# The selective stage: normalisation on ScalarE, modulation on GpSimd, and the network's end in the next turn

## The reference, cut to what is computed here

```python
def _L3_xattn_ref(x_text, x_vision, ...):        # x_text = _layernorm(x)
    Q = (x_text @ Wq).reshape(Bb, Tt, H, DH)      # 4 heads of 32
    K = (x_vision @ Wk).reshape(Bb, Gg, H, DH)
    scores = jnp.einsum('bthd,bghd->bhtg', Q, K) / np.sqrt(DH).astype(np.float32)
    topv, topi = jax.lax.top_k(scores, K_TOP)     # 32 of 120
    probs = jax.nn.softmax(topv, axis=-1)
    attn = jnp.zeros_like(scores).at[bi, hi, ti, topi].set(probs)
    attn_mean = attn.mean(axis=1)
    V = x_vision @ Wv
    c_t = jnp.einsum('btg,bgd->btd', attn_mean, V)
    x = layernorm(x_text, g_norm_in, b_norm_in)
    scale_in, shift_in = jnp.split(c_t @ W_film_in + b_film_in, 2, axis=-1)
    x = x * (1.0 + mod_gate * scale_in) + mod_gate * shift_in
    y = s4d(x, log_dt, A_re, A_im, C_re, C_im, D_skip)
    scale_out, shift_out = jnp.split(c_t @ W_film_out + b_film_out, 2, axis=-1)
    y = y * (1.0 + mod_gate * scale_out) + mod_gate * shift_out
    xt = x_text + y
    h = layernorm(xt, g_ffn, b_ffn)
    h = jax.nn.gelu(h @ W1 + b1, approximate=False) @ W2 + b2
    xt = xt + h
    return layernorm(xt, g_norm_out, b_norm_out)
```

## Time and profile before

| | us |
|---|---|
| median of 3 runs (lowest, highest) | 4631.86 (4628.33, 4635.73) |
| the profiled execution | 4636.67 |
| its span | 4634.9 |
| TensorE busy in the span | 4151.4 (90%) |
| VectorE busy | 3322.0 (72%) |
| ScalarE busy | 2232.4 (48%) |
| GpSimd busy | 529.9 (11%) |

### The profile page before, as it was taken

How to read it: one execution, slowest core, us unless ns; L and a number is a source line. 1 busy time by engine, 2 the same in 40 slices (tenths; PEclk the granted TensorE clock), 3 DMA queues, 4 the chain that set the end, 5 groups by cost and what they waited for, 6 DMA issues and landing times. The chain is left out here.

```text
span 4634.9 us, 72082 instructions
## 1 busy us (share of the span) xinstructions
PE 4151.4 (90%) x23376; PEld 3267.9 (71%) x23376; DVE 3322.0 (72%) x7934; ACT 2232.4 (48%) x5314; POOL 529.9 (11%) x982
## 2 busy tenths in 40 slices
PE   7998988999699999999999999999985888888686
PEld 6876766777387877778777777777863665656555
DVE  6985667666677777777777677777767888876455
ACT  3545655555365565655555555565531232322332
POOL 1331010111500000000000000001142111111300
PEclk9998999999799999999999999999975999989699
DMA  3000000000000000000000000000020000000101
GB/s 93 0 0 37 0 1 0 0 0 0 18 3 2 4 2 4 1 2 4 2 4 2 4 1 2 4 2 2 1 72 1 1 1 0 0 1 0 40 0 36
DMA packets 33797, 40.58 MB, mean 9 GB/s; under 512 B 5550, under 2 KB 30006, under 8 KB 33466
## 3 DMA queue, kind: packets, MB, share of 16 engines
q1 hardware_dynamic: 32732, 37.03, 2.7%
q10 hardware_dynamic: 800, 0.33, 0.0%
HBM read 32.90 MB, written 4.19 MB: 8 GB/s over the span
## 5 line engine op out<-in xcount | busy, mean ns | idle before, releaser
L1739 ACT ACTIVATE global_prob_t_high<-psum 128x512 fp32r<-128x512 f32 x960 | 570.7, 601 | 588.9 <-PE psum L1853 588.9
L1647 DVE TENSOR_TENSOR global_prob_t_low<-psum,global_prob_t_high 128x512 fp32r<-128x512 f32 x960 | 657.2, 690 | 251.0 <-ACT global_prob_t_high L1739 237.0
L1653 DVE TENSOR_REDUCE global_top<-psum 128x1 f32<-128x480 f32 x1024 | 666.9, 658 | 110.8 <-PE psum L1813 106.3
L1811 PE MATMUL psum<-global_prob_t_high,global_v_low 128*128 128x512 f32 x960 | 455.6, 475 | 1.0
L1811 PE MATMUL psum<-global_k_high,global_q_low 128*128 128x480 f32 x1024 | 390.6, 381 | 17.4 <-ACT spare L1760 14.8
L1813 PE MATMUL psum<-global_k_high,global_q_high 128*128 128x480 f32 x1024 | 391.1, 382 | 0.0
L1812 PE MATMUL psum<-global_k_low,global_q_high 128*128 128x480 f32 x1024 | 388.9, 380 | 0.0
L1812 PE MATMUL psum<-global_prob_t_low,global_v_high 128*128 128x512 f32 x960 | 379.7, 396 | 0.0
L1813 PE MATMUL psum<-global_prob_t_high,global_v_high 128*128 128x512 f32 x960 | 379.6, 395 | 0.0
L1760 ACT ACTIVATE spare<-psum,global_bias 128x480 f32<-128x480 f32 x512 | 337.8, 664 | 16.5 <-DVE global_bias L1656 15.1
L1760 ACT ACTIVATE global_prob<-psum,global_bias 128x480 f32<-128x480 f32 x512 | 337.9, 663 | 1.2
(11 more groups left out here) (455 smaller groups left out, 8593.3 us busy)
## 6 DMA issues: line engine op xcount, KB each, us to landing
x_res<-in_x SPq DMA_DIRECT2D x8, 512.0 KB, 9.8
moe_we<-in_expert_t SPq DMA_DIRECT2D x8, 512.0 KB, 7.6
out<-x_res SPq DMA_DIRECT2D x4, 1024.0 KB, 8.5
cho_wqkv<-in_L_ffn_Wqkv SPq DMA_DIRECT2D x2, 1536.0 KB
self_ctx_t<-in_ctx_t SPq DMA_DIRECT2D x2, 1440.0 KB, 13.6
sel_w<-in_L_xattn_W SPq DMA_DIRECT2D x2, 1024.0 KB, 11.2
global_ctx_t<-in_ctx_t SPq DMA_DIRECT2D x1, 1440.0 KB
sel_ctx_t<-in_ctx_t SPq DMA_DIRECT2D x1, 1440.0 KB
```

The lines of the kernel that those rows point to most:

```text
L1647: dve.tensor_tensor(dst, psum, high.bitcast(F32), ALU.subtract).then_inc(ready.sem, 1)
L1653: ins = dve.tensor_reduce(top[:, c:c + 1], w.psum[:, c, 0:chunk], AX.X, ALU.max)
L1739: act.activation(dst, psum, ACT.Copy).then_inc(ready.sem, 1)
L1811: pe.matmul(to, lhs_low, rhs_high, start=start, stop=False)
```

## The change

In one turn there is now a fourth sequence, done (now - 1), and one more turn at the end.

- **Layernorm of x, h and the last one.** VectorE still makes the statistics. GpSimd makes the root and beside it `offset` = -mean * root. ScalarE then normalises with one activation a tile (`Identity`, scale = root, bias = offset). It was VectorE before.
- **Second layernorm (g_norm_in).** The statistics of the normalised rows are no longer taken: their mean is nought, and their variance is var * root^2, from which GpSimd takes the second root (`rstd_of_normed`). VectorE multiplies xl by it and by the gain, and adds the bias row.
- **Modulation of u** (two operations of 128x512): GpSimd in place of VectorE, ahead of the sum with shift_out in its order.
- **The network's end** (sum over W2's result, statistics, normalisation, gain, sum into x): at the start of the next turn on VectorE, in place of the end of this one.
- **TensorE's order**: k and v, transposes of the mean, forward, transposes of xl, c, q, backward, scores, film_in, transposes of h, W1, W2, film_out.
- **ScalarE's order**: the exponentials ahead of the gelus.

```diff
+            iteration((2 * t + 2, 0), (2 * t + 1, 1), (2 * t, 0), 2 * t - 1)
+            iteration((2 * t + 3, 1), (2 * t + 2, 0), (2 * t + 1, 1), 2 * t)
+        iteration(None, (B - 1, 1), (B - 2, 0), B - 3)
+        iteration(None, None, (B - 1, 1), B - 2)
+        iteration(None, None, None, B - 1)
...
     def scale_rows(pool, chain, half, n):
-        _, mean_var, r = norms[half]
+        _, mean_var, r, offset = norms[half]
         need(pool, f"stats_{half}", n)
+        pool.tensor_tensor(offset[:, :], mean_var[:, :, 0], minus_one[:, :], ALU.mult)
         chain.link(pool.tensor_tensor(r[:, :], mean_var[:, :, 1], w.eps[:, :], ALU.add))
-        pool.tensor_tensor(r[:, :], r[:, :], w.neg_half[:, :], ALU.pow).then_inc(sig(f"rstd_{half}").sem, 1)
+        chain.link(pool.tensor_tensor(r[:, :], r[:, :], w.neg_half[:, :], ALU.pow))
+        pool.tensor_tensor(offset[:, :], offset[:, :], r[:, :], ALU.mult).then_inc(sig(f"rstd_{half}").sem, 1)
+
+    def scale_normed_rows(pool, chain):
+        _, mean_var, r, _ = norms["a"]
+        r2 = rstd_of_normed[:, :]
+        chain.link(pool.tensor_tensor(r2, mean_var[:, :, 1], r[:, :], ALU.mult))
+        chain.link(pool.tensor_tensor(r2, r2, r[:, :], ALU.mult))
+        chain.link(pool.tensor_tensor(r2, r2, w.eps[:, :], ALU.add))
+        pool.tensor_tensor(r2, r2, w.neg_half[:, :], ALU.pow).then_inc(sig("rstd_normed").sem, 1)
...
                 if F:
                     i, p = F
+                    need(pool, "u_base", i)
+                    need(pool, "film_in_ready", i)
+                    chain.link(pool.tensor_tensor(u_in[p], u_in[p], mods_in[:, :, 0:D], ALU.mult))
+                    pool.tensor_tensor(u_in[p], u_in[p], mods_in[:, :, D:2 * D],
+                                       ALU.add).then_inc(sig("u_ready").sem, 1)
                     need(pool, "film_out_ready", i)
...
+                if done is not None:
+                    need(dve, "ffn_psum", done)
+                    link(dve.tensor_tensor(xt, w.psum[:, 4:6, 0:D], xt, ALU.add))
+                    dve.engine_nop().then_inc(sig("ffn_kept").sem, 1)
+                    stats("b", 2 * done + 1, lambda s: xt[:, s, :])
                 if T:
-                    stats("a", 2 * T[0], x_tile(T[0]))
+                    stats("a", T[0], x_tile(T[0]))
+                if done is not None:
+                    need(dve, "yn_ready", done)
+                    link(dve.tensor_tensor(y, y, rows["g_norm_out"][:, :].unsqueeze(1).to_broadcast([P, LANES, D]),
+                                           ALU.mult))
+                    need(dve, "x_biased", done)
+                    dve.tensor_tensor(both_tiles(done), both_tiles(done), y, ALU.add).then_inc(sig("x_updated").sem, 1)
...
+            def normalise(half, x, to):
+                _, _, r, offset = norms[half]
+                for s in range(LANES):
+                    ins = act.activation(to[:, s, :], x(s), ACT.Identity, scale=r[:, s:s + 1], bias=offset[:, s:s + 1])
+                return ins
```

200 lines of the change are left out of this document (94 added, 106 removed).

## The result

The changed kernel takes 4577.85 us (median of four runs, 4572.24 to 4580.45) against 4632.74 us (4628.33 to 4635.73) for the kernel before: a ratio of 0.9881, 95% interval 0.9864 to 0.9898. It is 54.9 us, or 1.2%, faster. The forecast was 4617 us with a range of 4597 to 4640, so the direction was right and the gain was 3.7 times the expected one (54.9 against 14.9).

A forecast was written before the change was run, and what follows sets the result against it. Bound: a chain back and forth between TensorE and VectorE. From 4636.67, -17 for 13 turns, -4 ahead and +6.5 at the end give 4622.2 us profiled, so a forecast of 4617 us, range 4597 to 4640.

The forecast's parts named there:

- The removed waits: TensorE's waits for ffn_kept, xl and ScalarE's copies go; its matmuls stay the same, 36.50 us a turn.
- The cover over h: Scores and film_in on TensorE stand over h's normalisation, some 5.3 us, with 0.1 to 0.3 us to spare.
- The wait at the head: TensorE stands 3.3 us before kv each turn, behind film_out's copies, base and the context's copy.
- W2: TensorE's W2 waits 1.15 us a turn because ScalarE's exponentials now stand ahead of the gelus.
- Backward's: A term of 0.15 us in the sum for TensorE's turn at full clock, 41.8 us.
- The clock: After the head's wait, kv, mean's transposes and forward run at 1.2 GHz: 3.4 us lost, turns of 45.2.
- First and last turns: Outside the 13 full turns: -4 us ahead of the first W1, +6.5 us at the end.
- (a): Rival: the head costs no more clock than now; turns of 43.9 us or less, median 4595 to 4607; chance 0.20.
- (b): Rival: ScalarE's table loads, exponentials and gelus become the bound; turns 45.8 to 46.5, median 4625 to 4635; chance 0.23.
- (c): Rival: 1.2 GHz lasts past forward over c, q and backward; 12 us of it make median 4651; chance 0.12.
- (d): Rival: VectorE still sets the head, yn or products late; 1 us late makes turns of 46.2; chance within (b)'s.
- room of 0.7 us at full clock: At the head, the products are through 11.1 us after film_out and TensorE wants the spectrum at 11.8.

The follow-up runs named there:

- the run with seven fillers: The changed kernel with 7 extra matmuls of 128x256, their results never read, on TensorE ahead of k and v in each turn: 4558.85 us.

## Why the prediction was off, point by point

**What bounds the kernel** was read rightly: a chain that goes back and forth between TensorE and VectorE. The exponentials moved in the kernel before prove it more sharply than the waits did, since the 3.8 us given to VectorE alone brought 46.50 - 43.20 = 3.3 us a turn, part of it clock.

**The removed waits** were right in kind: ffn_kept, xl before its transposes, q's and c's copies, mean's copy and the 1.50's surplus over 0.69 are gone. Their size was off by 0.85 us a turn. "36.50 us are matmuls at 2.4 GHz" holds only with eight waits beside them, and the prediction carried the number over to a turn with three.

**The cover over h**, called 0.1 to 0.3 us thick, held: in the full-clock turns of the run with seven fillers no wait stands before h's transposes. The pair of normalisations took 1.09 us where 1.04 was reckoned, GpSimd's root 1.4 as reckoned.

**The wait at the head** was forecast at 3.3 us and measures 3.11, since the context's copy took 0.38 instead of 0.57. VectorE stood idle beside it here and was adding into x in the kernel before. **W2** was to begin 1.15 us late and begins 3826.34 - 3818.51 - 6.83 = 1.0 late, of which 0.66 is the bracket. **Backward's** 0.15 is gone. Together the waits are 4.46 and not 5.29, 0.83 us less.

**The clock** is the step that failed: "I take 3.4, the upper end". The price measured is 1.8 us a turn. The cause was right, as the filler shows; the size was taken from the longest stretch of the earlier trace rows, with the argument that matmuls now follow without a break. The runs say otherwise: behind the same wait of 3.11 a turn of the changed kernel lost 41.5 - 40.2 = 1.3 us or 43.2 - 40.2 = 3.0, and one with c put back lost nothing. The Trainium skill (TensorE: Matmul & The Clock Gate, HAM oscillation) has every tile begin at the lower clock when a wait recurs in each; the changed kernel's trace agrees, as its clock of 0.95 and its 1.92 us for kv's second half show, and five of the 13 turns of the run with c put back, at the same 3.11 us of wait, do not, nor do two of the 13 of the changed kernel with the exponentials last. What decides between the three prices stays open; no run here was made for it.

The kernel before already spoke against a price tied to the one long wait. Counted as a turn less its waits less 36.50, its five turns with a wait of 3.5 us lost 2.5 to 3.2 us, and the eight with no wait over 1.8 us lost between nothing and 3.1. One of those, the turn from 3660.62 to 3707.11, lost 3.1:

```profile
3687.58 0.66 PE L2676 MATMUL psum<-ident,spare 128*128 128x128 f32 x4 [1.79 <-DVEq L2489]
3688.92 1.92 PE L2681 MATMUL psum<-spare,sel_wq 128*128 128x256 f32 x4 [0.69 <-ACT spare L2574]
3690.64 4.56 PE L2690 MATMUL psum<-powers,sel_backward 128*128 128x256 f32 x16
```

q takes 1.92 us for 1.13 and backward 4.56 for 3.72 behind a wait of 1.79 and one of 0.69. The "2.84 us lost at least" behind a wait of 3.5 us doesn't hold either: behind the longest, 3.69 us in the turn from 3750.97, the same three groups take 1.12 + 2.07 + 4.20 us, 1.9 more than at full clock. The prediction had seen that turns with shorter waits lose up to some 3 us, and still priced the new turn by its longest wait.

The sum of the three: 0.85 + 0.83 + 1.6 = 3.3 us a turn, 43 us over 13 turns, which is the whole miss. All three came from taking numbers of the old turn into a turn of another shape, the clock's with the dearer end of its range, and all three erred on the same side. None of the three explains the miss alone; the clock's 1.6 is half of it.

**First and last turns.** -7.2 for -4 ahead, +8.5 for +6.5 behind (the prediction's own terms there, 4.0, 0.7 and 1.5, add up to 6.2 even before what the turn ahead of the last gains). Of the first, 1.5 us lie before the stage (kv's first matmul begins at 3517.58 instead of 3519.10). The programs of this study without fillers have it between 3512.46 and 3519.10, so that much is chance. In the last turns backward waits 3.04 and 5.79 us for the products and h's transposes 5.30. The last two are near what was reckoned (9.1 - 3.6 = 5.5, and 4.53 + 0.7 = 5.2). What was left out is the clock: in the last turn backward takes 6.22 us where it took 3.72:

```profile
4182.38 5.41 PE L2721 MATMUL psum<-powers,sel_backward 128*128 128x256 f32 x16 [3.04 <-DVE powers L2507]
...
4221.89 6.22 PE L2721 MATMUL psum<-powers,sel_backward 128*128 128x256 f32 x16 [5.79 <-DVE powers L2507]
```

**The rivals.** (a), the head costing no more clock than the turn paid before (2.1), is what happened, with a chance of 0.20; its own time of 4595 to 4607 was still 17 us too high, by the tails and the smaller waits. (b), a table load dearer than its row, did not come: the load takes 1.28 us and the next activation follows 0.01 us behind it, so the 2.66 us of the Trainium skill (ScalarE: Activation LUTs, What ACT_TABLE_LOAD costs) are not seen here. (c) needed more low clock than before, and there was less. (d) did not come: VectorE waits 4.86 us for yn and still has the products in time at low clock. Its "room of 0.7 us at full clock" was not there: in the full-clock turns of the run with seven fillers backward stands up to 0.15 us for them.

**What the prediction did not ask** is whether each part of the change pulls. The exponentials ahead of the gelus were costed as "worth nothing here, since VectorE will have room", and 1.15 us a turn against it. Those two sentences already say that this part should be left out, and the run without it is 17 us faster. And the head's wait was taken as given, though its row names an operation of 0.4 us that stood behind another for no reason of its data.

## What to carry to other kernels

When work leaves the engine that sets the pace, reread every order that was chosen to help it: an order that was worth 42 us before cost 17 afterwards. For each wait that a change creates, look at what its releaser does just before, and whether that must stand there; moving a copy of 0.4 us to the front of its queue was worth 34 us, and taking the rows that depend on least first, on all three engines, another 46. Count a removed wait with its tail, and price low clock from all turns, with and without such a wait, not from the longest.

## What the runs showed of the hardware

Matmuls whose results are thrown away made the kernel faster: seven of them in a wait of 3.1 us brought the clock of the stage from 0.95 to 1.00 and 1.8 us a turn. Twelve of them, 5.2 us, took about as much as they gave: turns of 41.97 against 41.94. The same wait of 3.11 us cost no clock at all in five of 13 turns of one kernel and 3 us in three of another's. Waits of 1.4 to 2.0 us cost none in 12 of 13 turns of the run with the copy first, but in the kernel before, with six other waits in the turn, one of 1.79 us was followed by 1.2 GHz in all turns but that of the earlier trace rows.

Each wait before a group of matmuls cost about 0.17 us beyond its bracket, as the four turns at full clock in the table above show on average; the wait before W2 alone cost 0.93 us at a bracket of 0.66.

Small operations of GpSimd took 0.72 and 1.24 us at 3915.19 and 3916.14 of the run with base behind the first root, while VectorE multiplied by g and made the residual sum, and 0.20 and 0.70 us elsewhere. VectorE's, too, grew: in the kernel before its residual sum over two tiles took 1.73 us at 3729.58, beside GpSimd's base (3729.24), and 0.88 in the run with the exponentials ahead, where GpSimd was idle beside it.
